# Preparing the first feed-forward's first inputs inside the first cross attention, and quantising its second weight matrix while its pipeline fills

## The reference

```
x = x + tanh(g_xattn[0]) * L0_xattn(layernorm(x), ctx, ...)   # stage 1
x = x + tanh(g_ffn[0])   * L0_ffn(layernorm(x), w1, b1, ...)  # stage 2
x = x + tanh(g_xattn[1]) * L1_xattn(...)                      # stage 3
x = x + tanh(g_ffn[1])   * L1_ffn(...)                        # stage 4

# stage 1: kv = ctx @ W_k.T + b_k; out = p @ kv; sim = out @ kv.T * scale
#          sim = layernorm_over_row(sim) * gamma + beta; result = softmax(sim)
# stage 2: h = gelu(silu(bitlinear(x, w1, b1))); h = layer_norm(h) * g + b
#          result = bitlinear(h, w2, b2)
# bitlinear: rms_norm(x), rows rounded to 8-bit integers by 127 / max|row|;
#            weights rounded to -1, 0, 1 by s = mean|w|: clip(round(w / s), -1, 1) * s
```

## Time and profile before

| | |
|---|---|
| median of 3 runs | 903.49 us (903.21 to 906.27) |
| the profiled execution | 903.19 us, span 901.4 us |
| mean granted TensorE clock | 0.899 of 2.4 GHz |
| DVE busy | 678.6 us, 75% |
| PE busy | 673.6 us, 75% |
| ACT busy | 610.7 us, 68% |
| POOL busy | 325.6 us, 36% |
| stage 1, `xattn0` | 0 to 110.2 us |
| stage 2, `ffn0` | 110.2 to about 359 us |

### The profile page before, as it was taken

The page is one execution under the profiler, slowest core; times in us unless marked ns, Lnnn a source line. Parts: engine busy times, 40 slices in busy tenths (PEclk is TensorE's granted clock), DMA queues, the critical chain, the costliest instruction groups (busy, mean ns, idle before and its releaser), DMA issues. The chain is left out here.

```text
span 901.4 us, 14255 instructions
## 1 busy us (share of the span) xinstructions
PE 673.6 (75%) x5262; PEld 371.7 (41%) x5262; DVE 678.6 (75%) x1140; ACT 610.7 (68%) x814; POOL 325.6 (36%) x355
## 2 busy tenths in 40 slices
PE   5853056767857757779989978899998377979785
PEld 2421023333423323446655545556355144545452
DVE  1569879999999997885893797556442488989983
ACT  2788459998977894588982886489362055656574
POOL 0012611446295556371671265113031023323332
PEclk9985578999887898679999998999999798989999
DMA  8800030000000000622320121123000000000001
GB/s 320 329 1 0 17 124 0 1 1 1 0 1 1 0 1 2 209 65 96 95 66 28 34 65 45 33 69 107 0 2 1 33 1 12 25 24 23 24 36 47
DMA packets 21761, 43.70 MB, mean 48 GB/s; under 512 B 3905, under 2 KB 8513, under 8 KB 20801
## 3 DMA queue, kind: packets, MB, share of 16 engines
q1 hardware_dynamic: 21696, 42.85, 13.8%
HBM read 38.61 MB, written 4.19 MB: 47 GB/s over the span
## 5 line engine op out<-in xcount | busy, mean ns | idle before, releaser
L1460 DVE TENSOR_REDUCE c_nmax<-c_s 128x1 f32<-128x384 f32 (+3 forms) x176 | 108.7, 633 | 83.5 <-PE c_s L1670 83.5
L1572 ACT ACTIVATE c_probs<-c_e 128x512 f32<-128x512 f32 (+1 forms) x176 | 94.5, 558 | 57.8 <-PE c_e L1700 56.8
L1395 POOL TENSOR_TENSOR c_psum<-c_probs 128x1536 f32<-128x1536 f32 x16 | 55.9, 3492 | 156.4 <-ACT c_probs L1572 156.4
L1168 PE MATMUL b_y<-w2q,b_q2T 128*128 128x512 bf16 x256 | 72.5, 438 | 51.4 <-ACT b_q2T L1093 25.8
L2098 PE MATMUL d_gu<-gateq,d_xqT 128*128 128x352 bf16 x512 | 93.1, 332 | 13.8 <-DVE d_h L1899 12.7
L1667 PE MATMUL c_s<-c_kT,c_qaT 96*128 96x128 f16 (+3 forms) x256 | 73.4, 320 | 22.5 <-DVE c_nmax L1460 20.2
L1142 PE MATMUL b_up<-shared,b_xqT 128*128 128x512 bf16 x256 | 73.5, 414 | 2.4 <-ACT b_h L1059 2.4
L1698 PE MATMUL c_e<-c_qaT,c_kT 98*128 98x512 f16 (+3 forms) x256 | 69.7, 306 | 3.3 <-ACT c_qaT L1559 2.8
L2027 ACT ACTIVATE d_sg<-d_gu,d_dq 128x352 f32<-128x352 f32 x64 | 35.4, 554 | 52.2 <-PE d_gu L2098 52.2
L2098 PEld LDWEIGHTS d_gu<-gateq,d_xqT 128*128 128x128 bf16 x512 | 49.4, 103 | 50.0 <-DVE d_h L1899 19.0
L1168 PEld LDWEIGHTS b_y<-w2q,b_q2T 128*128 128x128 bf16 x256 | 25.6, 108 | 90.0 <-issue 36.5
(11 more groups left out here) (232 smaller groups left out, 1836.0 us busy)
## 6 DMA issues: line engine op xcount, KB each, us to landing
c_stage<-in_gateT SPq DMA_DIRECT2D x16, 704.0 KB, 4.0
c_stage<-in_downT SPq DMA_DIRECT2D x6, 768.0 KB, 4.7
xs<-in_x SPq DMA_DIRECT2D x4, 1024.0 KB, 17.3
a_wf<-in_w1T SPq DMA_DIRECT2D x2, 2048.0 KB, 16.0
a_wf<-in_w2T SPq DMA_DIRECT2D x2, 2048.0 KB, 20.9
out<-xs SPq DMA_DIRECT2D x16, 256.0 KB, 2.0
a_ctxT<-in_ctxT SPq DMA_DIRECT2D x1, 1024.0 KB, 4.9
b_ln_g<-in_ln_g SPq DMA_DIRECT2D x1, 1024.0 KB, 4.8
```

Source lines behind the costliest of these rows:

```text
L1168: last = nc.tensor.matmul(y_ps[:], q2T[:, n % 2, c, :], w2q[:, c, :], start=(c == 0), stop=(c == IC - 1))
L1395: nc.gpsimd.tensor_tensor(psum[:], region(slot, 0)[:, :, P:], region(slot, 1), ALU.add).then_inc(psum_ready, 1)
L1460: nc.vector.tensor_reduce(nmax[:, G % 2, i, n:n + heads], s_ps[u % 2][:, 0:heads * (i + 1) * P].rearrange("p (n k) -> p n k", n=heads), ax ...
L1572: nc.scalar.activation(probs[:, G % 2, at:at + width], e_ps[fill % 3][:, 0:width], ACT.Exp).then_inc(e_read, 1)
```

## The change

The input preparation of `ffn0` becomes a class `Entry` with the same instructions in three parts: `centred`, `quantised` (up to the integers) and `terms` (`dq` and the three bf16 terms). Its tiles, the five slots (`hidden`, formerly `h`), `winv` and the chunk semaphores are allocated ahead of both stages. In `xattn0`:

- DVE calls `entry.centred` and `entry.quantised` of pair b after `finished(2 * b)` for b = 0 and 1, and `entry.terms` of pair 0 in batch 3 ahead of `variances(7)`. POOL clears the room of the terms and takes the two powers. `weight_sum(0)` comes behind the second of these.
- w1's chunks stay in a tile `w1f`; w2's four chunks are loaded into slots 1 to 4 of `hidden`; `xT`, `wkT` and `junk` are put into room that is already there.
- DVE clips 1, 0, then 2 before `finished(6)`, and 3 after it. POOL scales and stores chunks 1 and 2 only, each in two instructions of 1024 columns. ACT scales 0, 3 and 4, and stores 0 and 3.

In `ffn0`, w2's chunks are finished at its start: POOL scales 6 and 7, ACT scales 5 after its two first copies, and DVE clips and stores 4, does `terms(1)`, and clips and stores 6, 5 and 7, all ahead of its loop. silu of tiles 1 to 4 waits until its slot's chunk is stored, and the first product with w2 until all are.

```diff
@@ xattn0, DVE
+                if b == BATCH - 1:
+                    dve.wait_ge(xq_cleared, 1)
+                    entry.terms(dve, 0)
                 variances(2 * b + 1)
...
                 if b == 3:
                     clip(1)
+                    clip(0)
                     weight_scale(1)
                     clip(2)
                 finished(2 * b)
+                if b < 2:
+                    dve.wait_ge(x_ready, 2 * b + 2)
+                    entry.centred(dve, b)
+                    entry.quantised(dve, b)
                 if b == 1:
                     weight_sum(0)
...
-            clip(0)
             clip(3)
             finished(PAIRS - 1)
-            for k in range(4, W_CHUNKS):
-                clip(k)
@@ xattn0, POOL
             def scale(k):
-                nc.gpsimd.tensor_scalar(wf[:, k, :], ...)
+                for at in (slice(0, INNER // 2), slice(INNER // 2, INNER)):
+                    last = nc.gpsimd.tensor_scalar(w1f[:, k, at], w1f[:, k, at], winv[:, 0:1], MAGIC, ALU.mult, ALU.add)
...
+                if p == 1:
+                    entry.cleared(pool).then_inc(xq_cleared, 1)
+                    entry.scale(pool, 0)
+                if p == 3:
+                    entry.scale(pool, 1)
                 if p == 5:
                     scale(1)
                     scale(2)
-            store(0)
             store(1)
-            scale(5)
-            store(3)
-            store(4)
-            store(6)
+            store(2)
@@ xattn0, ACT
+            store(0)
             scale(4)
-            store(2)
-            scale(6)
-            scale(7)
-            store(5)
-            store(7)
+            store(3)
@@ ffn0, DVE
-            dve.wait_ge(psetup, 1)
-            centred(0)
-            quantised(0)
-            centred(1)
-            quantised(1)
+            clip(4)
+            store(4)
+            entry.terms(dve, 1)
+            for k in (6, 5, 7):
+                clip(k)
+                store(k)
@@ ffn0, POOL
-            nc.gpsimd.memset(xq[:, :, DIM:], 0.0).then_inc(psetup, 1)
-            inputs_scale(0)
-            inputs_scale(1)
+            scale(6)
+            scale(7)
@@ ffn0, ACT
+                if 1 <= n < HS and k == 0:
+                    act.wait_ge(chunk_stage[CH + n - 1], 3)
...
             gather(0)
             gather(1)
+            scale(5)
@@ ffn0, PE
+                if n == 0:
+                    for c in range(2 * k, 2 * k + 2):
+                        pe.wait_ge(chunk_stage[CH + c], 3)
```

More of the change, by code:

```diff
@@ L297, in flamingo @@
         vec0_loaded = sem("vec0_loaded", w0)
+        hidden = sb("hidden", [P, 5, INNER], where=w0)
+        winv = sb("winv", [P, 2], where=w0)
+        winv_ready = sem("winv_ready", w0)
+        chunk_stage = [sem(f"chunk_stage{k}", w0) for k in range(W_CHUNKS)]
+        entry = Entry(nc, sb, sem, w0, locals())
         with ExitStack() as ph:
@@ L371, in xattn0, with chunk @@
     v_ready, exp_ready, x_ready = s("v_ready"), s("exp_ready"), s("x_ready")
[L372 to L376, removed]
+    wabs_ready, wtot_ready, wtot_done = s("wabs_ready"), s("wtot_ready"), s("wtot_done")
     MAGNITUDES = (((), (0, 1)), ((2,), (3, 4)), ((5, 6), (7,)), ((), ()))
-    targets = ([w1q[:, k, :] for k in range(CH)]
-               + [w2q[:].rearrange("p c n -> p (c n)")[:, k * INNER:(k + 1) * INNER] for k in range(W_CHUNKS - CH)])
+    def chunk(k):
+        return w1f[:, k, :] if k < CH else hidden[:, 1 + k - CH, :]
     def cols(p):
@@ L625, in magnitude @@
                     act.wait_ge(wabs_ready, k)
[L626 removed]
+                nc.scalar.activation(junk, chunk(k), ACT.Abs, accum_out=wabs[:, k:k + 1]).then_inc(wabs_ready, 1)
             def scale(k):
                 act.wait_ge(winv_ready, k // CH + 1)
[L630 removed]
+                nc.scalar.activation(chunk(k), chunk(k), ACT.Copy, scale=winv[:, k // CH:k // CH + 1],
                                      bias=MAGIC).then_inc(chunk_stage[k], 1)
@@ L769, in ffn0 @@
     scale2 = t("scale2", [P, 1])
[L770 to L774, removed]
+    xq, dq1 = entry.xq, entry.dq
     xqT = t("xqT", [P, 4, CH + 1, P], bf16)
-    h, h2 = t("h", [P, HS, INNER]), t("h2", [P, H2S, INNER])
+    h, h2 = g["hidden"], t("h2", [P, H2S, INNER])
     junk1, junk2 = t("junk1", [P, INNER], bf16), t("junk2", [P, INNER], bf16)
@@ L820, in _ @@
         def _(dve):
[L821 to L834, removed]
-                    small.mark(nc.vector.tensor_scalar(xc[:, k, :], xs[:, n + k, :], mv[:, n + k, 0:1], None, ALU.subtract))
@@ new lines, in _, with inputs, clip, store @@
+            small = entry.small
+            def inputs(p):
+                entry.quantised(dve, p)
+                entry.terms(dve, p)
+            def clip(k):
+                dve.wait_ge(chunk_stage[k], 1)
+                nc.vector.tensor_scalar(h[:, 1 + k - CH, :], h[:, 1 + k - CH, :], MAGIC + 1.0, MAGIC - 1.0,
+                                        ALU.min, ALU.max).then_inc(chunk_stage[k], 1)
+            def store(k):
+                dve.wait_ge(chunk_stage[k], 2)
+                nc.vector.tensor_scalar(w2_flat[:, (k - CH) * INNER:(k - CH + 1) * INNER], h[:, 1 + k - CH, :],
+                                        -MAGIC, None, ALU.add).then_inc(chunk_stage[k], 1)
@@ L946, in _ @@
                 n = 2 * p
-                centred(p + 2)
+                entry.centred(dve, p + 2)
                 sloped(n)
@@ L960, in _ @@
                 residual(n - 1)
-                quantised(p + 2)
+                inputs(p + 2)
                 second_half(n)
@@ L1025, in _ @@
                 deviation(n)
-                inputs_scale(p + 2)
+                entry.scale(pool, p + 2)
                 output_scale(n - 1)
@@ L1094, in first_half, with scale @@
                                      ACT.Copy, bias=-LIFT).then_inc(first_turned, 1)
+            def scale(k):
+                nc.scalar.activation(h[:, 1 + k - CH, :], h[:, 1 + k - CH, :], ACT.Copy, scale=winv[:, 1:2],
+                                     bias=MAGIC).then_inc(chunk_stage[k], 1)
             gather(0)
             gather(1)
+            scale(5)
             for p in range(PAIRS + 1):
```

192 lines of the change are left out of this document (121 added, 71 removed).

## The result

The changed kernel took **891.6 us** (median of 4 runs, 891.13 to 892.4) against 903.51 (4 runs, 903.21 to 906.27): ratio 0.985, 95% interval 0.982 to 0.988. The forecast was 888.8, in a range from 883 to 894.5. Run again later, beside more runs of the kernel before, it took 890.3 against 905.1 (23 runs, 902.1 to 909.1), ratio 0.984 (0.982 to 0.986). So the gain is 11.9 us by the first set of medians and 14.8 by the second; the forecast said 14.7.

What follows compares the result with a forecast made beforehand. DVE's queue was taken to set the length of both stretches; 9.5 (end of `xattn0`) + 3.6 (`ffn0`'s start) + 1.6 (`rstd` waits) = 14.7 us off 903.49 gave 888.8 us, 8-in-10 range 883 to 894.5.

Steps and rivals of the forecast that it cites:

- Rival 3: TensorE's clock falls in `ffn0`; slower only if its mean is below 0.65; at 0.62, 913 us; chance 0.03.
- Parts 1 to 3: Additions in `xattn0` ahead of DVE's first clip make that clip 1.4 us later, at 88.3 us.
- Part 3: `terms(0)` in batch 3 of `xattn0`, partly covered by idle time: +0.9 us (0.8 to 1.7).
- Part 1: Inputs prepared in DVE's idle time in batches 0 and 1 of `xattn0`: 0.2 us late (0 to 0.5).
- part 2: POOL's scales of chunks 1 and 2 in halves, in `xattn0`: +0.3 us (from -1.0 to +1.0).
- Part 4: Rest of `xattn0` from the first clip: 8.4 us of DVE work plus 3.6 of lock; block ends 9.5 us earlier.
- T: Start of `ffn0`: 110.2 us before, forecast 100.7.
- the lock: DVE and POOL hold each other up on SBUF; priced at 0.95 us per POOL instruction of 1024 columns.
- Part 5: Start of `ffn0`: `sloped(0)` at T + 18.4, 3.6 us less than before, with DVE later than `nmu(0)`.
- Rival 1: DVE gets through the lock first, in `xattn0` and `ffn0`'s start: gain 20.4 us, 883 us; chance 0.18.
- Part 6: First two tiles of `ffn0`: DVE's waits for `rstd` go, 1.6 us.
- Nothing takes it back: To 345 us no DVE wait could end the gain; `ffn0`'s tail and stages 3 and 4 move unchanged.

Runs made afterwards that it cites:

- after_again: The changed kernel run again unaltered; 890.3 us.
- before_again: The kernel before the change run again unaltered; 905.0 us.
- entry_only: Against the kernel before: only the first two pairs' inputs prepared in `xattn0`, all weight chunks still quantised there; 897.5 us, ratio 0.990.
- w2_only: Against the kernel before: only w2's chunks finished at the start of `ffn0`, inputs of pairs 0 and 1 prepared there too; 899.8 us, ratio 0.993.
- pool_whole: The changed kernel with POOL's scales and stores of chunks 1 and 2 in one instruction of 2048 columns each; 891.2 us.
- act_scales6: The changed kernel with ACT scaling chunk 5 in `xattn0` and 6 in `ffn0`, POOL only 7 there; 887.1 us, ratio 0.982.
- act_scales67: The changed kernel with ACT scaling chunk 5 in `xattn0`, 6 and 7 in `ffn0`, and POOL none there; 888.7 us, ratio 0.984.
- warm_after: The changed kernel with 32 fp32 products of 128x128 ahead of PE's first wait for data; 891.4 us.
- terms_wait_d: The changed kernel with `terms` waiting for the value d only, not the last write of the integers; 888.6 us, ratio 0.980.
- changed: The changed kernel in its first set of runs, against the kernel before; 891.6 us, ratio 0.985.
- act67_d: The changed kernel with ACT scaling chunks 5, 6 and 7 and `terms` waiting for d only; 888.6 us, ratio 0.982.
- act6_d: The changed kernel with ACT scaling chunks 5 and 6 and `terms` waiting for d only; 887.4 us, ratio 0.980.
- The warmed pair: Kernel before and changed kernel, both with 32 fp32 products ahead of PE's first wait for data; 906.7 and 891.4 us.

## Why the prediction was right, and where it was off

The mechanism stands, and the time lies in the range. Point by point, measured in after_again against before_again unless said otherwise:

- *DVE bounds both stretches, and what its loop gains at its start it keeps.* Right in the main: 13.4 us at `sloped(0)`, 14.2 at `sloped(15)`, 12.5 at stage 3. Rival 3 (the clock below 0.65 throughout) didn't come: 0.89 and 0.86.
- *Parts 1 to 3, 1.4 us.* Mis-sized: the first clip came 2.1 us later, at an equal start 2.5. Part 3 was near (0.7 in entry_only, whose lag behind before_again goes from 1.1 to 1.9; forecast 0.9). Part 1 cost 1.1 instead of 0.2: in before_again DVE's idle time before the two variances is 2.75 and 1.56 us, not 3.96 and 1.55 as in the earlier trace rows. The cover of one profiled execution was taken for that of all. The rest is the halves (part 2), some 0.6 instead of 0.3.
- *Part 4, 12.0 us from the first clip to the end.* 11.6 to T, with the block's end in it; the lock cost 2.7, not 3.6, since POOL gave way too (its four halves took 6.4 us, where 3.8 would do). T came at 100.56, forecast 100.7: that is luck, since the two errors cancel. In w2_only and pool_whole the same ledger holds.
- *Part 5, T + 18.4.* T + 17.6. The store takes 1.23 us (forecast 1.25), the lock 3.3 to 3.4 instead of 3.7, as act_scales6 and act_scales67 show by taking it away. DVE was the later one, as said. The Trainium skill (SBUF — State Buffer, "Who interferes with whom") has the loser blocked for the whole of the other's instruction; a clip that takes 2.93 us beside one POOL instruction and 1.22 without it agrees. Rival 1, that DVE gets through first, is refuted at this place, and partly true in `xattn0`.
- *Part 6, 1.6 us.* Right here: from `sloped(0)` to `sloped(2)` 25.4 us for 27.1. In warm_after and pool_whole it is 25.8, with a wait of 0.51 us for `rstd` left.
- *Nothing takes it back.* This step failed, by some 2.7 us. From `sloped(2)` to `sloped(15)` the loop lost 1.0 us. 0.6 of it went to the wait at the head of `terms`, at 0.12 a pair (shown by terms_wait_d). I had called the instructions the same and overlooked that the split function waits for one more of them. 0.3 us went between `sloped(3)` and `sloped(4)`, to a wait for POOL's `rstd`, and 0.1 to the wait for PE ahead of `sloped(13)`. And the tail of `ffn0`, from `sloped(15)` to stage 3, takes 24.94 us instead of 23.25. The prediction moved it as it was, as if a block end stood ahead of it; there is none, and in it DVE waits for PE.

The 0.3 us are the lock once more, now against POOL. after_again, and below it before_again:

```profile
152.71 2.35 DVE L960 SCALAR_TENSOR_TENSOR b_h<-hidden,b_nmu,b_ln_g 128x2048 f32<-128x2048 f32 x1
152.88 2.23 POOL L1066 TENSOR_SCALAR b_va<-b_css 128x1 f32<-128x1 f32 x1 [2.67 <-ACT b_junk L1147]
155.84 2.35 DVE L968 SCALAR_TENSOR_TENSOR b_h<-b_h,b_rstd,b_ln_b 128x2048 f32<-128x2048 f32 x1 [0.18 <-POOL b_rstd L1068]
```

```profile
167.39 0.57 POOL L996 TENSOR_SCALAR b_va<-b_css 128x1 f32<-128x1 f32 x1 [2.06 <-ACT b_junk L1076]
167.83 2.35 DVE L888 SCALAR_TENSOR_TENSOR b_h<-b_h,b_nmu,b_ln_g 128x2048 f32<-128x2048 f32 x1
```

In after_again ACT's squares end just after DVE has begun `sloped(3)`. The first of POOL's two instructions for `rstd`, one value per row, then takes 2.23 us, to the end of `sloped(3)`, and `affine(3)` waits for the second. In before_again it came 0.44 us ahead of `sloped(3)` and took 0.57.

The tail is PE's. after_again, and below it before_again:

```profile
333.63 2.33 PE L1247 MATMUL b_y<-w2q,b_q2T 128*128 128x512 bf16 x8 [3.21 <-ACT b_q2T L1164]
335.76 1.06 PE L1234 MATMUL b_t<-ident_b,hidden 128*128 128x128 bf16 x8
336.61 2.75 PE L1247 MATMUL b_y<-w2q,b_q2T 128*128 128x512 bf16 x8
```

```profile
347.76 1.89 PE L1168 MATMUL b_y<-w2q,b_q2T 128*128 128x512 bf16 x8 [2.84 <-ACT b_q2T L1093]
349.49 0.61 PE L1158 MATMUL b_t<-ident_b,b_h 128*128 128x128 bf16 x8
349.93 1.89 PE L1168 MATMUL b_y<-w2q,b_q2T 128*128 128x512 bf16 x8
```

Busy time by stretch around these groups, with the columns of the first table of stretches above (PEclk is the granted clock), after_again and then before_again:

```profile
333.00:341.00 8.00, 6.89 (x36) 3.57 (x37) 5.57 (x8) 3.40 (x4) 5.53 (x8) 0.79 0.00 0
335.30:338.00 2.70, 2.70 (x14) 1.57 (x13) 1.96 (x3) 1.10 (x2) 2.48 (x3) 0.50 0.00 0
```

```profile
346.00:354.00 8.00, 5.77 (x38) 3.08 (x39) 6.71 (x10) 4.53 (x6) 6.74 (x8) 1.00 0.00 0
```

From the first start to the last end the same three groups take 5.7 and 4.1 us: the difference is that of the tails. The granted clock is 1.00 throughout in before_again, and 0.50, so 1.2 GHz, for 3.4 us in after_again, while PE works. This is not firmly the change's. The traces with the long tail (changed, after_again, entry_only, w2_only, terms_wait_d, act67_d, 24.9 us) all have this fall of the clock there. The eight others (the three of before, warm_after, pool_whole, act_scales6, act_scales67, act6_d, 23.3 us) have none. Just ahead of the first of these groups PE had been idle for 3.2 to 3.6 us in the long ones and for 2.1 to 3.2 in the short ones. What makes the clock fall in one execution and not in the other is not shown. Rival 3 had this mechanism, but in the loop and with 24 us.

The forecast missed the first median by 2.8 us. The marks of the first trace, with the forecast's steps laid on the profiled execution of before, place a little more than that: `sloped(0)` was 1.1 us late (2.8 at the start, 1.1 more in parts 1 to 3, less what the chain of that execution of before had lost and parts 4 and 5 gave back), the loop 1.5 (203.6 us to `sloped(15)` where 202.1 were forecast; 0.7 of it is DVE's wait for PE ahead of `sloped(13)`, 1.4 us for 0.7 in that execution of before), the tail 1.7, and the rest of the kernel came 0.3 early. That is 3.9 us in spans; the traced run was 0.8 us above its median and that of before 0.3 below its own, which leaves 2.8. That the forecast gain of 14.7 meets 14.8 in the second set of medians is in part luck: in the traces of before_again and after_again only 12.5 us of 14.7 stand at stage 3, and 2.3 come in stages that the change doesn't touch. The warmed pair, with equal tails, has 14.1 at stage 3.

## What to carry to other kernels

An engine that bounds a steady loop should reach it with its queue empty: look for the filling of the pipeline, count what the bounding engine does there and what it waits for, and move work that nobody waits for into it, and work that others wait for out of it. The two moves are worth more together than apart (13.4 us against 6.6 and 2.0 at the loop's start), since each alone meets the limit that the other lifts. And a cover read from one execution is a sample: 1.2 us of it was gone in the next. An engine that bounds the loop doesn't bound its tail: look there for what another engine does.

## What the runs showed of the hardware that was not expected

- In the first 20 us one group of fp32 products took 1.94 us in one execution and 1.07 in another, and a second group 5.20 and 3.67, while the records give a granted clock of 1.00 for both; products put in front bring the short durations (1.02 for 2.05). In this stretch the durations tell the rate, the column doesn't.
- A POOL instruction of 2048 columns, 1.90 us alone, held a DVE clip for 1.7 us. Cutting POOL's work in halves changed nothing in sum. The other way round, a POOL instruction of one value per row took 2.23 us beside a DVE instruction of 2048 columns, and 0.57 ahead of one.
- A DVE instruction that waits for the one right ahead of it (128x1024 to bf16, then 128x2) started 0.12 us later than without the wait (0.73 for 0.61).
- The granted clock fell to 0.50 for 3.4 us in the midst of PE's last groups in six of fourteen traces, which made the stage 1.7 us longer.
